# Second attention: two heads from different halves of TensorE's rows in each step

## The reference

```python
# x [2*2, 256, 256], y = context [4, 256, 128]; H = 16 heads of HD = 16; the last 16 keys are "dca" keys
def _attn(q, k, v):
    s = jnp.einsum('bhqd,bhkd->bhqk', q, k) * SCALE
    p = jax.nn.softmax(s, axis=-1)
    return jnp.einsum('bhqk,bhkd->bhqd', p, v)
q = _ln((x @ Wq + bq).reshape(b, s1, H, HD), qn_w, qn_b)
k = _ln(kv[..., :HD], kn_w, kn_b); v = kv[..., HD:]           # 240 keys
ctx = _attn(qT, kT, vT)                                        # softmax over the 240 keys
ctx_dca = _attn(qT, k_dcaT, v_dcaT)                            # own softmax over the 16 dca keys
out = (ctx + ctx_dca).reshape(...) @ Wo + bo
```

## Time and profile before

| | |
|---|---|
| median of 3 runs | 1162.64 us (1160.04 to 1165.0) |
| profiled execution | 1156.74 us, of it span from first to last instruction 1155.3 us |
| TensorE busy | 1021.8 us, 88% of the span |
| VectorE, ScalarE, GpSimd busy | 742.0, 481.9, 257.5 us |
| mean granted TensorE clock | 0.95 of full |
| second attention, first to last score product | 778.8 to 945.8 us |
| score products (line 1652) | 256 matmuls, 65.4 us busy, 397 ns each |

### The profile page before, as it was taken

How to read it: one execution, slowest core, us unless ns; L and a number is a source line. 1 busy time by engine, 2 the same in 40 slices (tenths; PEclk the granted TensorE clock), 3 DMA queues, 4 the chain that set the end, 5 groups by cost and what they waited for, 6 DMA issues and landing times.

```text
span 1155.3 us, 14112 instructions
## 1 busy us (share of the span) xinstructions
PE 1021.8 (88%) x4772; PEld 701.6 (61%) x4772; DVE 742.0 (64%) x1808; ACT 481.9 (42%) x1158; POOL 257.5 (22%) x206
## 2 busy tenths in 40 slices
PE   5766778999999999999999999999989998987556
PEld 2222233568999998899856555656656765544444
DVE  4888995235666668666755465558757765477653
ACT  3554352136666665666611111125545452132331
POOL 2445562121111112111100011811732100010110
PEclk9887889999999999999999999999999899989677
DMA  5000001001110131110012221111000003211200
GB/s 214 0 1 0 0 1 46 1 28 42 42 42 28 45 117 42 42 42 28 1 42 69 81 69 55 55 55 42 1 1 2 1 1 119 83 41 28 80 19 18
DMA packets 16335, 46.90 MB, mean 41 GB/s; under 512 B 2300, under 2 KB 3462, under 8 KB 15624
## 3 DMA queue, kind: packets, MB, share of 16 engines
q1 hardware_dynamic: 15400, 44.67, 11.6%
q10 hardware_dynamic: 864, 1.34, 0.3%
HBM read 44.96 MB, written 1.05 MB: 40 GB/s over the span
## 4 chain that ended last, share of the span: by engine, by line
PE 73%; DVE 8%; POOL 4%; issue 3%; ACT 2%; POOLq 0%; DVEq 0%; ACTq 0%
PE psum L1409 15%; PE psum L1428 7%; PE psum L906 5%; PE psum L1098 5%; PE psum L1109 5%; PE psum L1078 4%; PE psum L1652 4%; PE psum L767 4%; PE psum L909 3%; PE psum L1089 2%; PE psum L1951 2%; PE psum L930 2%; POOL arena L393 2%; PE psum L778 2%; PE psum L1935 2%
## 5 line engine op out<-in xcount | busy, mean ns | idle before, releaser
L1409 PE MATMUL psum<-xT,arena 128*128 128x512 f32 x400 | 183.4, 601 | 7.6 <-DVE arena L1600 1.9
L1409 PEld LDWEIGHTS psum<-xT,arena 128*128 128x128 f32 x400 | 75.4, 192 | 85.0 <-issue 83.2
L988 POOL TENSOR_TENSOR arena<-arena,mhalf 128x8 f32<-128x8 f32 x32 | 53.5, 1672 | 274.1 <-DVE arena L973 274.1
L1494 DVE TENSOR_TENSOR arena<-psum,arena 128x512 f32<-128x512 f32 x50 | 34.5, 691 | 110.0 <-PE psum L1409 110.0
L1463 ACT ACTIVATE arena<-psum 128x512 f32<-128x512 f32 x50 | 29.7, 596 | 174.6 <-PE psum L1409 174.6
L393 POOL TENSOR_TENSOR arena<-arena 128x512 f32<-128x512 f32 x64 | 82.5, 1311 | 79.0 <-DVE arena L695 76.2
L1210 DVE SCALAR_TENSOR_TENSOR X<-psum,arena,X 128x256 f32<-128x256 f32 x128 | 55.9, 478 | 68.0 <-PE psum L1109 68.0
L1428 PE MATMUL psum<-arena 128*128 128x256 f32 x400 | 95.2, 380 | 2.7 <-DVE arena L1494 2.7
L450 PE MATMUL psum<-arena,ident 128*128 128x512 f32 x128 | 77.6, 703 | 22.5 <-POOL arena L393 22.3
L1428 PEld LDWEIGHTS psum<-arena 128*128 128x128 f32 x400 | 75.3, 190 | 32.1 <-issue 21.4
L1506 DVE SCALAR_TENSOR_TENSOR X<-psum,arena,X 128x256 f32<-128x256 f32 x192 | 83.2, 478 | 8.5 <-PE psum L1428 8.1
(11 more groups left out here) (279 smaller groups left out, 1981.2 us busy)
## 6 DMA issues: line engine op xcount, KB each, us to landing
arena<-in_moe SPq DMA_DIRECT2D x50, 384.0 KB, 3.0
arena<-in_w SPq DMA_DIRECT2D x32, 384.0 KB, 3.0
arena<-in_w SPq DMA_DIRECT2D x2, 1024.0 KB, 6.7
arena<-in_gu SPq DMA_DIRECT2D x1, 1280.0 KB, 6.3
X<-in_x SPq DMA_DIRECT2D x2, 512.0 KB, 9.7
arena<-in_ctok SPq DMA_DIRECT2D x2, 512.0 KB, 7.1
arena<-in_fsideT SPq DMA_DIRECT2D x1, 1024.0 KB, 4.8
arena<-in_fside SPq DMA_DIRECT2D x1, 1024.0 KB, 6.9
```

The costliest lines, as they stand in the source:

```text
L1409: mm = nc.tensor.matmul(bank[b], m.W[:, slot, which, c * P:(c + 1) * P], k.xT[:, c, cols], start=c == 0, stop=c == DC - 1)
```

## The change

The pair of a step is chosen anew. Step g takes chunk c = g // 4 and index i = g % 4, and its two heads are head i of the chunk's upper half (rows 0 to 63) and head i of its lower half (rows 64 to 127). The four products are issued alternately, first queries of both heads and then second queries of both. In the products with the values both copies out of PSUM are awaited ahead of the first product, and the two heads alternate as well. Their results go to two quarters of the output partitions, i and (i + 2) % 4. This places heads at other positions, so the sums and reciprocals are written at two positions that are 6 or 2 apart, and the value biases and the rows of Wo are permuted on the host. The wait for GpSimd's copies stands at g % 4 >= 2 and no longer at odd g.

```diff
+def pair_heads(g):
+    return g // 4, g % 4
+
+def pair_places(g):
+    c, i = pair_heads(g)
+    one, two = 8 * c + i, 8 * c + 4 + (i + 2) % 4
+    return one, two, slice(one, two + 1, two - one)
...
     pe.wait_ge(*at("a2_Qb", b, g // 4))
-    if g % 2:
+    if g % 4 >= 2:
         pe.wait_ge(*at("a2_Qc", b, g // 4))
-    for e in range(2):
-        h = 2 * g + e
-        c, r = h // 8, h % 8 // 4 * 64
-        for j in range(2):
-            mm = nc.tensor.matmul(bank[2 * u + e][:, j * S:(j + 1) * S],
-                                  m.Qb[r:r + 64, h % 4, c, j * P:(j + 1) * P], m.Kb[r:r + 64, c, :],
-                                  start=True, stop=True)
-        mm.then_inc(*tick("a2_S", s, e))
-        k.free[2 * u + e] = [("a2_E", s)]
+    c, i = pair_heads(g)
+    for j in range(2):
+        for e in range(2):
+            rows = slice(64 * e, 64 * e + 64)
+            mm = nc.tensor.matmul(bank[2 * u + e][:, j * S:(j + 1) * S], m.Qb[rows, i, c, j * P:(j + 1) * P],
+                                  m.Kb[rows, c, :], start=True, stop=True)
+            if j:
+                mm.then_inc(*tick("a2_S", s, e))
+                k.free[2 * u + e] = [("a2_E", s)]
...
-        for w in range(2):
-            h = 2 * g + w
-            pe.wait_ge(*(at("a2_PTv", s) if w else at("a2_PTa", s)))
-            o = 6 * 512 + h // 4 * S
-            for c in range(2):
-                mm = nc.tensor.matmul(k.psum[h % 4 * 32:(h % 4 + 1) * 32, o:o + S], m.Vb[:, c, h, :],
-                                      m.PT[:, 2 * u + w, c, :], start=c == 0, stop=c == 1)
+        pe.wait_ge(*at("a2_PTa", s))
+        pe.wait_ge(*at("a2_PTv", s))
+        chunk, i = pair_heads(g)
+        for c in range(2):
+            for w in range(2):
+                region, quarter = 2 * chunk + w, (i + 2 * w) % 4
+                o = 6 * 512 + region * S
+                mm = nc.tensor.matmul(k.psum[quarter * 32:(quarter + 1) * 32, o:o + S],
+                                      m.Vb[:, c, 8 * chunk + 4 * w + i, :], m.PT[:, 2 * u + w, c, :],
+                                      start=c == 0, stop=c == 1)
...
-        nc.vector.reciprocal(m.inv[:, :, 2 * g:2 * g + 2, :],
-                             m.sums[:, :, 2 * g:2 * g + 2, :]).then_inc(*tick("a2_inv", s))
+        nc.vector.reciprocal(m.inv[:, :, pair_places(g)[2], :],
+                             m.sums[:, :, pair_places(g)[2], :]).then_inc(*tick("a2_inv", s))
...
+    placed = (16 * np.array(places)[:, None] + np.arange(16)).reshape(-1)
...
-            "bq": a["L2_xattn_bq"], "bv": bv2, "bvd": a["L2_xattn_bkv_dca"][D:],
+            "bq": a["L2_xattn_bq"], "bv": bv2[placed], "bvd": a["L2_xattn_bkv_dca"][D:][placed],
...
-    out["wo2"] = tiles(a["L2_xattn_Wo"])
+    out["wo2"] = tiles(a["L2_xattn_Wo"][placed])
```

More of the change, by code:

```diff
@@ L1661, in a2_exponentials_act @@
     g, u = s % STEPS, s % 2
+    places = pair_places(g)
     v = k.psum[:, 2 * u * 512:(2 * u + 2) * 512].rearrange("p (a t) -> p a t", t=S)
@@ L1670, in a2_exponentials_act @@
         nc.scalar.activation(pr[:, a, 0:KM], v[:, a, 0:KM], ACT.Exp, bias=m.nb[:, u, a:a + 1],
-                             scale=m.SCALE, accum_out=m.sums[:, a % 2, 2 * g + a // 2, 0:1])
+                             scale=m.SCALE, accum_out=m.sums[:, a % 2, places[a // 2], 0:1])
     nc.scalar.activation(pr[:, :, KM:S], pr[:, :, KM:S], ACT.Exp, scale=m.SCALE).then_inc(*tick("a2_E", s))
@@ L2074, in attention2_dve @@
         dve.wait_ge(*at("a2_E", s))
-        nc.vector.tensor_reduce(m.sums[:, :, 2 * g:2 * g + 2, 1].rearrange("p j h -> p h j"),
+        nc.vector.tensor_reduce(m.sums[:, :, pair_places(g)[2], 1].rearrange("p j h -> p h j"),
                                 m.Pr[:, u, :, KM:S].rearrange("p (h j) t -> p h j t", h=2), AX,
@@ L2952, in layout @@
     bk2, bv2 = (v.reshape(-1) for v in joined(a["L2_xattn_bk"], a["L2_xattn_bv"]))
+    places = [0] * 16
+    for g in range(8):
+        for e, place in enumerate(pair_places(g)[:2]):
+            places[place] = 8 * pair_heads(g)[0] + 4 * e + pair_heads(g)[1]
+    placed = (16 * np.array(places)[:, None] + np.arange(16)).reshape(-1)
     out = {}
```

## The result

The changed kernel takes 1151.6 us (median of 6 runs, 1146.92 to 1154.31); the kernel before took 1161.69 on the same occasions (6 runs). The ratio is 0.9911, with a 95% interval of 0.9891 to 0.993, so 8 to 13 us faster. The profiled execution has a span of 1145.4 us, 9.9 less than before. Run a second time beside two variants, the changed kernel took 1149.75 against 1160.77, ratio 0.9902 (0.9885 to 0.992).

The account below looks back on a forecast made before the run. TensorE was taken to bound plain steps at 3.94 us, with ScalarE's 3.25 next. Stretch gains 1.7 + 0.25 + 2.0 + 1.4 + 1.8 + 1.7 + 2.2 = 11.05 off 1162.64 gave 1151.6 us; range 1145 to 1161.

Parts of the forecast that it names:

- to the hand-over from GpSimd: Attention from 778 to 845 us: nothing while VectorE is full, 1.7 us beside projections, 0.25 us under GpSimd's chain.
- three plain groups: Steps after 855 us: gains of 0.85, 0.68 and 0.68, less 0.2 for VectorE's query copies, 2.0 us.
- first three of the third batch: Next batch's first three score groups: gains of 0.85, 0.56 and nothing, with VectorE's round at 3.9 us; 1.4 us.
- second three: That batch's next three groups: 0.85 + 0.68 + 0.68, less 0.2 for query copies and 0.2 for bank 5; 1.8 us.
- the slow group: Score group at 912.91 us, 3.57 us long at the lower clock: four distances of 0.43 saved, 1.7 us.
- last three: Final three groups, 936 to 949 us, with nothing else on VectorE: 0.85 + 0.68 + 0.68, 2.2 us.
- 0.2 for bank 5, which VectorE frees later: Deduction of 0.2 us from the 1.8 us gain of that batch's second three groups, for VectorE freeing bank 5 later.
- no overlap: Score products: row halves served one after another, whole groups stay 1.92 us; 2.6 us slower, 1165.2 us; chance 0.12.
- a pause at each change: Score products: each change of row half costs 0.1 us and nothing overlaps; 8.6 us slower, 1171.2 us; chance 0.05.
- program order: Score products: matmuls start and end strictly in order, 0.64 us saved per group; 10.0 us gained, 1152.6 us; chance 0.10.
- All of it lands: Whole attention: ScalarE and VectorE don't bind, 19 groups give 0.85 us each; 17 us gained, 1145.6 us; chance 0.05.
- clock rival: TensorE's added idling brings one more low-clock stretch, leaving 7.65 us gain, 1155.0 us, chance 0.08; one fewer gives 1.7 more.

## Why the prediction was right

The time came out at the forecast, 1151.6, and the mechanism as it was priced. That the two agree to the tenth is luck: the forecast took 11.05 off a median of 1162.64, and measured were 10.1 off 1161.69 and, the second time, 11.0 off 1160.77. The mechanism is this: the score group takes what one head alone takes (forecast 1.07 plus the way through the array, measured 1.14), plain steps come 3.26 apart, half groups give 0.1 at most, the products with the values stay at 1.06, and GpSimd's chain still hands over with no gap (TensorE's wait for it grew by 1.2 us, 5.8 for 4.6, where 2 were forecast). But the terms of the sum did not all hold. Stretch by stretch, gains in the traces, from the start of the attention, each stretch up to the start of the work named, on the chain:

| stretch | forecast | measured |
|---|---|---|
| to the hand-over from GpSimd (66.36, then 65.74) | 0 + 1.7 + 0.25 | 0.6 |
| three plain groups, to the last products with the values of the second batch | 2.0 | 1.8 |
| first three of the third batch, to the projection | 1.4 | 0.9 |
| second three, to line 251 | 1.8 | 0.2 |
| the slow group, to step 26 | 1.7 | 2.8 |
| last three | 2.2 | 2.3 |
| sum | 11.05 | 8.6 |

- The first term lost 1.3 to the clock: the scores at 794.60 and the transposes behind them took 0.9 and 0.4 longer than at full speed. With these the term is 1.9, as forecast. In the kernel with the copy moved in five kinds of step, whose trace has the full clock there, the hand-over comes at 63.36, but the moved copy has its share in that. The prediction read VectorE's 9.97 of 10 as VectorE's own work; some 1.6 of it are the one instruction of 1.76 (at 792.38 there) that ends with GpSimd's operation.
- The first three of the third batch: VectorE's round was longer than the 3.9 I gave it. Step 18 came 4.52 after step 17. Two instructions of two elements per partition took 0.35 and 0.60 us on the chain (line 1703 at 874.10 and 875.20), where they take 0.1 otherwise. GpSimd adds the two halves of the finished batch at that time, and each of the two instructions ends with one of its operations, as in the stretch before 793.
- "0.2 for bank 5, which VectorE frees later" is the term that was mis-sized. It measured 1.7 (a wait of 1.82 for 0.10 before), nearly the whole of that stretch. I had left out what else VectorE does in this step, the normalisation of four tiles for the next block, which the kernel before hid. VectorE's timeline of the changed kernel:

```profile
893.97 1.93 DVE L239 TENSOR_SCALAR xn<-X,mv,rstd 128x256 f32<-128x256 f32 x4
...
897.66 0.68 DVE L2097 COPY arena<-psum 128x512 f32<-128x512 f32 x1
```

  Line 239 takes 1.93 from 893.97 on, the copy out of bank 5 begins at 897.66, and line 251 at 898.44. In the kernel before the same four tiles took 1.33; here the last two took 0.70 each for 0.41, beside two operations of GpSimd (894.32 to 895.75). With the copy moved ahead in this step, TensorE's waits for line 251 fell from 4.2 to 2.0 us.
- The slow group: the forecast kept the low clock there. In this trace it is gone at 907.63 (1.11 for 3.57) and stands at 899 to 903 instead, at 0.59; the earlier trace rows show it from 913 on. That gave 1.1 more than the term.

Sum and time agree less closely than the figures suggest. The stage gives 8.6 in the first pair of traces and 7.7 in the second trace of the changed kernel, and the medians differ by 10 to 11. The part outside the attention, whose code is the same, differs as well: the attention starts at 776.19 for 778.76, and from its last transposes to the end the changed kernel needs 1.3 more. Both traces are of quick executions (1156.74 under a median of 1161.69, and 1146.92 under 1151.6). Two kernels with the same steps as before, the one with only the values alternated and the one without the dca exponential, have stages of 173.9 and 175.6 us in their traces, and the granted clock stays low longer in them. How much of the missing 2 us is the clock and how much is the stage of a typical execution of the kernel before, these traces can't tell.

The rivals: no overlap and a pause at each change are refuted by the group of 1.14 us, in either order; program order by the kernel with the loops exchanged. "All of it lands" is refuted by the plain steps at 3.26 and the 9.2 us of waits for ScalarE. The clock rival happened in a weaker form, as a low stretch that moved and a new one at 794. Low-clock stretches inside the attention were one of the signs of being wrong that the prediction set itself, and it came true: the first cost 1.3 us and the moved one gave 1.1 back, so that the sum hardly felt it.

## What to carry to other kernels

When one engine of a pipelined loop gets faster, don't divide the gain evenly over the steps: write down the round of every other engine for each kind of step, with all that stands in its queue in that step, also the work of the next block that was hidden until now. Here 28 us less work on TensorE gave 10 us, and moving one copy ahead of another head's maxima gave 8 more, because a good part of the waits that were left came from the order of VectorE's work and not from its amount. Look also at what an engine is busy with: an instruction of 128 x 2 elements that takes 1.76 us for its usual 0.17 is not at work all that time. Two float32 products over 64 rows each run side by side if their operands lie in different row halves, so pair such products, whatever their order in the program.

## What the runs showed of the hardware

- Two heads in different row halves take 1.14 us for 8 float32 matmuls of 256 columns, two in the same half 1.99. With the four of one head ahead of the four of the other in the program it is 1.14 as well, so matmuls of one half overtake those of the other. The Trainium skill, in "TensorE: Matmul & The Clock Gate", Part 3, has matmuls start and end in strict program order; by that I estimate 1.14 and three distances of 0.21 more, some 1.8 us for the group, and the measurement decides against it here.
- Shorter waits than I expected were followed by the lower clock: after 2.41 us of waiting up to 793.26 (and 2.93 up to 785.51) the scores at 794.60 took 2.01, and after 1.82 us up to 898.44 the granted clock from 899 to 903 was 0.59. In the kernel before the same places had waits of 1.7 and 0.1 and no slow group behind them; but a kernel with its steps (only the values alternated) did have one at the first place in its trace, so it isn't the overlap alone that brings it.
- An inverse root by GpSimd's power operation on 128 x 32 elements takes 5.44 us, a multiplication of the same shape 0.25.
- VectorE's negated maximum of 128 x 2 elements, 0.17 us by itself, took up to 1.76 beside GpSimd. All 15 that took over 0.2 us, in the traces of before and changed, ended 0.02 to 0.03 us after an operation of GpSimd. Beside the power operation (5.4 us) they took 0.17.
